# A graph-attention layer: 32 quads written out in place of a hardware loop, waits on constants

## The reference

```python
q = (x @ Wq.T).reshape(B, N, 12, 32)
k = (x @ Wk.T).reshape(B, N, 12, 32)
v = (x @ Wv.T + bv).reshape(B, N, 12, 32)
a = einsum('bnhd,bmhd->bhnm', q, k) * 384 ** -0.5 + adj[:, None]
a = where(all(a == 0, axis=-1)[..., None], -inf, a)      # a row of zeros
a = nan_to_num(softmax(a, axis=-1))                      # gives a row of zeros
o = einsum('bhnm,bmhd->bnhd', a, v).reshape(B, N, 384)
y = x + o @ Wo.T + bo
out = (y - mean(y)) / sqrt(var(y) + 1e-5)                # x, out: (128, 128, 384) float32
```

## Time and profile before

| | |
|---|---|
| median of 3 runs | 1311.45 us |
| the profiled execution | 1316.24 us |
| its span, first to last instruction | 1314.1 us |
| TensorE matmul busy | 1239.2 us, 94% |
| VectorE, ScalarE, GpSimd busy | 80%, 78%, 65% |
| mean granted clock of TensorE | 0.991 |

### The profile page before, as it was taken

How to read it: one execution, slowest core, us unless ns; L and a number is a source line. 1 busy time by engine, 2 the same in 40 slices (tenths; PEclk the granted TensorE clock), 3 DMA queues, 4 the chain that set the end, 5 groups by cost and what they waited for, 6 DMA issues and landing times.

```text
span 1314.1 us, 39607 instructions
## 1 busy us (share of the span) xinstructions
PE 1239.2 (94%) x11742; PEld 1059.2 (81%) x11742; DVE 1047.5 (80%) x5094; ACT 1025.6 (78%) x4007; POOL 858.8 (65%) x775
## 2 busy tenths in 40 slices
PE   9999999999999999999999999999998999999986
PEld 7887887878878787888878888788787887878875
DVE  5887887878788787887878878788787888878886
ACT  6887877868778777887878788788777887878784
POOL 2766766657667666676666666667666666667675
PEclk9999999999999999999999999999999999999998
DMA  6021202222122121122220221211222112212110
GB/s 220 22 82 67 74 27 80 74 67 74 33 74 74 67 80 59 42 80 70 71 75 26 80 75 66 75 43 64 75 72 75 54 46 81 74 67 74 33 43 31
DMA packets 58829, 87.64 MB, mean 67 GB/s; under 512 B 3680, under 2 KB 54624, under 8 KB 58720
## 3 DMA queue, kind: packets, MB, share of 16 engines
q1 hardware_dynamic: 58720, 86.65, 19.5%
HBM read 61.47 MB, written 25.17 MB: 66 GB/s over the span
## 4 chain that ended last, share of the span: by engine, by line
POOL 55%; issue 30%; PE 9%; DVE 2%; POOLq 2%; ACT 1%; DMA 0%; DVEq 0%; SPq 0%
POOL probs L668 24%; POOL fold L661 18%; POOL x_sb L654 9%; POOL inv_std L675 5%; PE turn_bank L217 2%; PE turn_bank L219 2%; PE turn_bank L218 2%; PE pT_bank L254 1%; PE score_bank L241 1%; PE turn_bank L266 1%; POOLq L660 1%; POOLq L667 1%; DVE neg_a L525 1%; ACT probs L402 0%; DMA xT_raw<-xT_dram 0%
## 5 line engine op out<-in xcount | busy, mean ns | idle before, releaser
L402 ACT ACTIVATE probs<-neg_a,neg_max 128x128 f32<-128x128 f32 x1536 | 596.4, 396 | 47.3 <-DVE neg_max L525 46.0
L668 POOL TENSOR_TENSOR probs<-probs,row_scale 128x768 f32<-128x768 f32 x256 | 376.5, 1471 | 193.6 <-DVE row_scale L553 193.6
L661 POOL TENSOR_TENSOR fold<-neg_a 128x384 f32<-128x384 f32 x256 | 271.0, 1059 | 195.3 <-DVE neg_max L525 195.3
L525 DVE CUSTOM_DVE_ANT_0 neg_a<-score_bank,adj_sb 128x128 f32<-128x128 f32 x1536 | 333.2, 285 | 0.0
L409 ACT ACTIVATE pT<-pT_bank 128x384 f32<-128x384 f32 x512 | 220.7, 484 | 105.3 <-PE pT_bank L254 105.0
L402 ACT ACTIVATION_READ_ACCUMULATOR probs<-neg_a,neg_max 128x1 f32 x1536 | 300.1, 195 | 0.0
L217 PE MATMUL turn_bank<-xT_hi,w_hi 128*128 128x512 f32 x576 | 241.0, 418 | 29.6 <-DVE xT_lo L501 28.7
L219 PE MATMUL turn_bank<-xT_hi,w_lo 128*128 128x512 f32 x576 | 228.1, 396 | 0.0
L218 PE MATMUL turn_bank<-xT_lo,w_hi 128*128 128x512 f32 x576 | 227.7, 395 | 0.0
L254 PE MATMUL pT_bank<-ident,probs 128*128 128x128 f32 x1536 | 219.8, 280 | 0.3 <-ACT pT L409 0.3
L254 PEld LDWEIGHTS pT_bank<-ident,probs 128*128 128x128 f32 x1536 | 176.1, 142 | 21.1 <-issue 1.2
(11 more groups left out here) (38 smaller groups left out, 2006.8 us busy)
## 6 DMA issues: line engine op xcount, KB each, us to landing
xT_raw<-xT_dram SPq DMA_DIRECT2D x32, 768.0 KB, 6.0
x_sb<-x_dram SPq DMA_DIRECT2D x32, 768.0 KB, 5.0
out_dram<-out_sb SPq DMA_DIRECT2D x128, 192.0 KB, 1.9
adj_sb<-adj_dram SPq DMA_DIRECT2D x32, 256.0 KB, 2.8
w_raw<-wq_t_dram SPq DMA_DIRECT2D x1, 576.0 KB, 5.6
w_raw<-wk_t_dram SPq DMA_DIRECT2D x1, 576.0 KB, 6.8
w_raw<-wv_t_dram SPq DMA_DIRECT2D x1, 576.0 KB, 7.9
w_raw<-wo_t_dram SPq DMA_DIRECT2D x1, 576.0 KB, 8.5
```

Of the source, the lines that this page charges most:

```text
L402: last = nc.scalar.activation(probs[b % 2][:, u, :], neg_a[b % 2][:, u, :], ACT.Exp, bias=neg_max[b % 2][:, u:u + 1], scale=-1.0, accum_ou ...
L525: last = nc.vector.tensor_tensor_reduce(out=neg_a[b % 2][:, u, :], in0=score_bank[trio][:, c * N:(c + 1) * N], in1=adj_sb[p][:, b, :], sca ...
L661: nc.gpsimd.tensor_tensor(fold[:, u, :], neg_a[b % 2][:, u, 0:N // 2], neg_a[b % 2][:, u, N // 2:N], ALU.add).then_inc(fold_done, 1)
L668: nc.gpsimd.tensor_tensor(probs[b % 2][:, u, :], probs[b % 2][:, u, :], row_scale[:, u].unsqueeze(2).broadcast_to([P, HALF, N]), ALU.mult) ...
```

## The change

`over_quads` becomes a Python loop over the 32 quads, so that every stream is straight code and every number in it a constant. With this the value computations on SyncE and the helper `wait_alone` go; its two callers wait for their semaphore alone. The order of the work, the buffers and the transfers are the same.

```diff
--- before.py
+++ after.py
@@ -144,14 +144,11 @@
 
             return (*ahead(j, p, (b + n) // QUAD), (b + n) % QUAD)
 
-        def over_quads(eng, quad):
-
-
-            with eng.Fori(0, QUADS // 2 - 1) as j:
-                for p in range(2):
-                    quad(j, p, True, True)
-            for p in range(2):
-                quad(QUADS // 2 - 1, p, p == 0, False)
+        def over_quads(quad):
+
+
+            for q in range(QUADS):
+                quad(q // 2, q % 2, q + 1 < QUADS, q + 2 < QUADS)
 
 
         @block.sync
@@ -188,9 +185,6 @@
             def quad(j, p, has_next, has_after):
                 q = 2 * j + p
 
-                for value in (*(QUAD * q + n for n in range(2 * QUAD + 1)), 16 * q + 16,
-                              CHUNKS * q + 2 * CHUNKS, q + 2):
-                    sp.compute_val(value)
                 if has_after:
                     sp.wait_ge(xT_lo_done, CHUNKS * q + 2 * CHUNKS)
                     load_xT(q + 2)
@@ -204,7 +198,7 @@
                 if has_after:
                     load_x(QUAD * q + 2 * QUAD, p)
 
-            over_quads(sp, quad)
+            over_quads(quad)
             for b in range(QUAD):
                 sp.wait_ge(out_stored[b], 16 * (QUADS + 1))
 
@@ -373,7 +367,7 @@
             transpose_probs(0, 0, 0, 0)
             transpose_probs(0, 0, 0, 1)
             pe.wait_ge(qk_done, QK + 2)
-            over_quads(pe, quad)
+            over_quads(quad)
 
 
         @block.scalar
@@ -482,19 +476,11 @@
             keep_pT(0, 0, 0, 3)
             for trio in range(2, 4):
                 exp_trio(0, 0, 1, trio)
-            over_quads(act, quad)
+            over_quads(quad)
 
 
         @block.vector
         def _(dve):
-            def wait_alone(semaphore, count):
-
-
-
-                dve.compute_val(count)
-                dve.wait_ge(b_loaded, 32)
-                dve.wait_ge(semaphore, count)
-
             def keep_xT_lo(j, p, c):
 
                 dve.wait_ge(xT_hi_done, CHUNKS * (2 * j + p) + c + 1)
@@ -519,7 +505,7 @@
 
                 if b == 0 and trio == 0:
                     dve.wait_ge(adj_loaded[p], 16 * (j + 1))
-                wait_alone(scores_psum, 4 * (QUAD * (2 * j + p) + b) + trio + 1)
+                dve.wait_ge(scores_psum, 4 * (QUAD * (2 * j + p) + b) + trio + 1)
                 for c in range(CHUNKS):
                     u = CHUNKS * trio + c
                     last = nc.vector.tensor_tensor_reduce(
@@ -574,7 +560,7 @@
                 nc.vector.bn_stats(stats[:, :], y_sb[:, :]).then_inc(ln_steps, 1)
 
             def mean_variance(j, p, b):
-                wait_alone(ln_steps, LN_STEPS * (QUAD * (2 * j + p) + b) + 1)
+                dve.wait_ge(ln_steps, LN_STEPS * (QUAD * (2 * j + p) + b) + 1)
                 nc.vector.bn_aggr(mean_var[:, :], stats[:, :]).then_inc(ln_steps, 1)
 
             def add_eps(j, p, b):
@@ -642,7 +628,7 @@
             mask_half(0, 0, 0, 1)
             mask_half(0, 0, 1, 0)
             mask_half(0, 0, 1, 1)
-            over_quads(dve, quad)
+            over_quads(quad)
 
 
         @block.gpsimd
@@ -707,7 +693,7 @@
                 fold_half(0, 0, 1, half)
             for half in range(2):
                 scale_half(0, 0, 1, half)
-            over_quads(pool, quad)
+            over_quads(quad)
 
 
 _OUT = "out_dram"
```

## The result

Four runs of the changed kernel took 1273.62 to 1275.66 us, median 1273.85; the kernel before, with one more run beside them, has a median of 1312.69 us. The ratio is 0.970, 95% interval 0.968 to 0.973. The profiled execution took 1274.01 us against 1316.24 before: 42.2 us less, where the prediction's sum was 43.3.

A forecast was written before the change was run, and what follows sets the result against it. TensorE was taken to set the pace, held up by VectorE's stalls at the loop's jumps. Jumps 39.2, waits 4.1 and the rest 0 gave 43.3 us off 1311.45, 1268.2; allowing for profiling, forecast 1270, range 1261 to 1284.

The forecast's parts named there:

- the prediction's sum: The total gain expected from the jumps, the waits on VectorE and the rest: 39.2 + 4.1 + 0 = 43.3 us.
- The price of a jump from whole periods, 2.80 us: Hardware loop over quads: quad pairs take 80.73 us with a jump, 77.93 without; 14 jumps cost 39.2 us.
- Rival (a): Only TensorE's idle for oT_lo and v_sb comes back, the rest is absorbed elsewhere: 29 us, 1282; chance 0.09.
- VectorE's jump is the cause, and the others' are free: At the loop's end VectorE stalls 2.95 us awaiting its jump target's fetch; TensorE passes its own jump without idle.
- rival (b): VectorE stalls there in straight code too; only the branch's 1.5 us and the aggregate's 4 us go: 1306; chance 0.04.
- The longer stream costs 0: Fetching all 32 quads as straight code, TensorE's included, costs 0 us; upper bound 94 us.
- Rival (c): Slower: TensorE starves for instructions in straight code; one 2.95 us stall a quad gives 1362; chance 0.05.
- The waits on VectorE, 4.1 us: Plain waits before VectorE's aggregates save 69 ns a graph, counted twice a quad over 30 quads: 4.1 us.
- VectorE has no other slack: From graph 1's y_sb to graph 2's two xT_lo VectorE never waits otherwise, so 69 ns counts twice a quad.
- xT_lo's wait about 0.8 us: Expected sign: TensorE's idle for xT_lo, 0.95 us a quad before, becomes about 0.8 us.
- From the profile to the median: Profiled execution 4.8 us above the median, perhaps from longer fetches under the profiler; hence median 1268.2 to 1273, forecast 1270.
- the sum's own 1268.2: The median of the kernel before less the whole summed gain: 1311.45 - 43.3 = 1268.2 us.

The follow-up runs named there:

- A hint alone: The kernel before with one branch prefetch hint at the head of VectorE's loop body, nothing unrolled: 1287.86 us, ratio 0.981.

## Why the prediction was right, step by step

- *The price of a jump from whole periods, 2.80 us.* Right for the profiled execution: VectorE alone written out takes 39.6 us off the same 29 quads, between the idle alone (29) and VectorE's pauses (46.5). Rival (a), which counted idle only, would have left 10 us. For a usual execution the price is somewhat high, as the last point says.
- *VectorE's jump is the cause, and the others' are free.* Shown for this body: VectorE alone written out gives what all together give, less the waits, and straight code has no pause, which puts rival (b) out. A hint alone takes 2.1 of 3.3 us away, so the fetch is most of it. The rule of the Trainium skill's "Runtime: NRT & Kernel Launch" (Instruction fetch mechanics) agrees; the Trainium skill's 108 ns for a compare-and-branch ("Advanced Engine Details and Errata", Control Flow Timing) was no guide to a jump of 2.9 us and more.
- *The longer stream costs 0.* Right. Rival (c) did not come: 34265 instructions, no pause at regular distances on any engine, in 1272 us. The fetches of TensorE's stream lengthened no pause even where VectorE still jumped.
- *The waits on VectorE, 4.1 us.* This term was mis-sized: 2.15 us, by the kernel with `wait_alone` put back. The pause did fall from 103 to 35 ns, but it counts once a quad and not twice (30 x 0.069 = 2.1 us). The step that failed is "VectorE has no other slack" between graph 1's y_sb and xT_lo. The changed kernel:

```profile
558.33 0.56 DVE L555 TENSOR_TENSOR y_sb<-turn_bank,x_sb 128x384 f32<-128x384 f32 x1
...
562.56 0.56 DVE L548 TENSOR_TENSOR oT_lo<-turn_bank,oT_hi 128x384 fp32r<-128x384 f32 x1
```

```profile
562.05 0.48 ACT L409 ACTIVATE oT_hi<-turn_bank 128x384 fp32r<-128x384 f32 x1
```

From y_sb to the oT_lo of graph 2 it is 4.23 us, and it was 4.23 before (577.15 to 581.38). oT_lo starts 0.03 us after ScalarE's oT_hi ends (562.53); VectorE's instructions overlap, so that no idle marks the wait. The first 69 ns ended there. From oT_lo to the end of xT_lo it is 7.12 us now and was 7.19: the second 69 ns arrived.
- *xT_lo's wait about 0.8 us.* 0.91: the same error. Behind it stood what the row couldn't tell: xT_lo was also about as early as GpSimd's scaling lets it be.
- *From the profile to the median.* I took the 4.8 us between the profiled execution and the median before as partly due to longer fetches under the profiler. No run shows that, and another cause is on record: the granted clock. Beside the experiments the kernel before ran 52 times more, with a median of 1314.0 us. Its 5 executions with a mean clock of 0.991 or less took 1316.4 us on average, its 11 with 0.997 or more 1312.3. The profiled one had 0.991 and its three falls of the clock: a dear execution, set against a low median of only three. (Longer pauses both take longer and bring the falls, so this doesn't part the two.) By the medians the change gave 1312.69 - 1273.85 = 38.8 us, 4.5 less than the sum: 2 from the waits, and about 2.5 from having priced the jumps in that execution. With the 1.2 us by which the median before came out higher than the three runs', the sum's own 1268.2 was 5.7 us low. The forecast of 1270 was only 3.9 us low because 1.8 us of the 4.8 were added back, for a reason that no run bears out; that part is luck.

## What to carry to other kernels

Here a pause for "issue" that came once a pass of a hardware loop was a jump whose target had to be fetched. Price such a pause by the period with and without it, and look at every engine's body: written out, it cost nothing here, while fewer and longer passes brought in an engine that was free. Mixing is not safe: the stream that got faster (SyncE's) started its load on top of another's fetch.

When a wait remains, look at what GpSimd does beside a late VectorE instruction with two SBUF inputs before moving what stands ahead of it; two reorderings gained 0 and 0.3%, and one that let the two take turns gained 2.6%.

## What the runs showed that I had not expected

Writing out SyncE alone made the kernel 2.1% slower, by moving one 768 KB load about 0.9 us nearer to VectorE's jump (pauses of 4.7 instead of 3.3 us). An instruction of VectorE with both inputs in SBUF took 1.0 us more beside a 1.47 us GpSimd instruction, with no idle shown in the profile. The granted clock fell to 1.2 GHz (0.50 in stretches of 2 us) behind all 27 pauses of VectorE over 4 us, in the three kernels that have such pauses, and behind three of the 14 of the kernel before, those of 3.56, 3.62 and 3.62 us; its longest, 3.76 us, had none.
